# Second graph product of a two-layer graph network: panels of 512 columns instead of 384, column scale and step weights moved

## What is computed

```python
def _L1_gnn_ref(node_feats, adj_matrix, W, b):
    n = adj_matrix.shape[0]
    adj = adj_matrix + jnp.eye(n, dtype=adj_matrix.dtype)
    deg = jnp.sum(adj, axis=1)
    dinv = jnp.where(deg > 0, deg ** (-0.5), 0.0)
    adj_norm = dinv[:, None] * adj * dinv[None, :]
    x = node_feats @ W.T + b
    mean = jnp.mean(x, axis=0, keepdims=True)
    std = jnp.std(x, axis=0, ddof=1, keepdims=True)
    x = (x - mean) / (std + 1e-06)
    return adj_norm @ x

def step(h, _):                       # 30 times, in _L1_ffn_ref
    h = h + 0.01 * jnp.tanh(h)
    h = h * jax.nn.sigmoid(h)
    h = _layernorm(h, ln_w, ln_b)
    h = jnp.einsum('bsc,dc->bsd', h, W) + b
    return (h, None)

x = x + _L0_gnn_ref(_layernorm(x), adj, L0_gnn_W)
x = x + _L0_ffn_ref(_layernorm(x)[None], ...)[0]
x = x + _L1_gnn_ref(_layernorm(x), adj, L1_gnn_W, L1_gnn_b)
x = x + _L1_ffn_ref(_layernorm(x)[None], ...)[0]
```

## Time and profile before

| | us |
|---|---|
| median of 3 runs (2027.34 to 2028.16) | 2027.58 |
| the profiled execution | 2028.44 |
| its span, first to last instruction | 2026.7 |
| first graph product and experts, to | 860 |
| standardising, from 860 to | 926.5 |
| second graph product, from 926.5 to | 1184.5 |
| steps, from 1184.5 to | 2026.7 |

### The profile page before, as it was taken

The page is one execution under the profiler, slowest core; times in us unless marked ns, Lnnn a source line. Parts: engine busy times, 40 slices in busy tenths (PEclk is TensorE's granted clock), DMA queues, the critical chain, the costliest instruction groups (busy, mean ns, idle before and its releaser), DMA issues. The chain is left out here.

```text
span 2026.7 us, 44601 instructions
## 1 busy us (share of the span) xinstructions
PE 1816.9 (90%) x12898; PEld 1741.1 (86%) x12898; DVE 1650.8 (81%) x4233; ACT 1339.8 (66%) x2735; POOL 1035.0 (51%) x1756
## 2 busy tenths in 40 slices
PE   6468899919999999778999969999999999999998
PEld 4368899919999999767999959989998989999997
DVE  4888977738999999657666649989899989999897
ACT  4323455516666666345566649888888988889885
POOL 4543325444555555440000027777777777777774
PEclk9778999959999999988999989999999999999999
DMA  8755579427888788425666400000000000000001
GB/s 292 241 191 180 167 208 198 111 90 240 232 231 233 232 236 230 101 76 203 187 184 183 121 6 2 2 3 2 3 1 3 2 3 1 1 1 0 3 1 69
DMA packets 101001, 226.46 MB, mean 112 GB/s; under 512 B 21313, under 2 KB 51779, under 8 KB 92364
## 3 DMA queue, kind: packets, MB, share of 16 engines
q1 hardware_dynamic: 86220, 206.33, 32.7%
q0 software_dynamic: 14592, 17.91, 4.6%
HBM read 204.43 MB, written 19.75 MB: 111 GB/s over the span
## 5 line engine op out<-in xcount | busy, mean ns | idle before, releaser
L2341 PE MATMUL ffn_psH<-ffn_w2h,ffn_vTh 128*128 128x256 f32 x1320 | 406.2, 308 | 11.4 <-DVE ffn_vTl L2408 11.3
L2341 PE MATMUL ffn_psH<-ffn_w2h,ffn_vTl 128*128 128x256 f32 x1320 | 374.9, 284 | 0.0
L2341 PE MATMUL ffn_psH<-ffn_w2l,ffn_vTh 128*128 128x256 f32 x1320 | 374.0, 283 | 0.0
L2448 POOL TENSOR_SCALAR ffn_vn<-ffn_vn,ffn_rstd,ffn_shift 128x256 f32<-128x256 f32 x540 | 299.7, 560 | 20.2 <-issue 0.3
L2415 DVE SCALAR_TENSOR_TENSOR ffn_u<-ffn_th,ffn_psH 128x512 f32<-128x512 f32 x390 | 265.2, 680 | 49.2 <-ACT ffn_th L2368 49.0
L2403 DVE BATCH_NORM_STATS2 ffn_stats<-ffn_vn 128x6 f32<-128x256 f32 x780 | 281.8, 404 | 14.2 <-issue 11.9
L2341 PEld LDWEIGHTS ffn_psH<-ffn_w2h,ffn_vTh 128*128 128x128 f32 x1320 | 252.3, 191 | 35.2 <-DVE ffn_vTl L2408 18.2
L2371 ACT ACTIVATE ffn_vn<-ffn_u 128x512 f32<-128x512 f32 x390 | 254.8, 653 | 15.2 <-DVE ffn_u L2415 15.2
L2341 PEld LDWEIGHTS ffn_psH<-ffn_w2l,ffn_vTh 128*128 128x128 f32 x1320 | 253.6, 192 | 0.0
L2341 PEld LDWEIGHTS ffn_psH<-ffn_w2h,ffn_vTl 128*128 128x128 f32 x1320 | 252.7, 191 | 0.0
L2322 PE MATMUL ffn_psT<-ident,ffn_vn 128*128 128x128 f32 x1560 | 234.4, 273 | 9.1 <-POOL ffn_vn L2448 3.8
(11 more groups left out here) (244 smaller groups left out, 5205.2 us busy)
## 6 DMA issues: line engine op xcount, KB each, us to landing
g_raw<-in_adjt SPq DMA_DIRECT2D x272, 384.0 KB, 3.8
moe_w1raw<-in_wall SPq DMA_DIRECT2D x33, 1024.0 KB
moe_w2raw<-in_wall SPq DMA_DIRECT2D x33, 1024.0 KB, 5.8
g_raw<-in_adjl SPq DMA_DIRECT2D x27, 256.0 KB, 2.7
moe_b<-in_eb SPq DMA_DIRECT2D x33, 128.0 KB, 4.8
xn_rows<-rt_hn SPq DMA_DIRECT2D x8, 384.0 KB, 4.5
x_rows<-x SPq DMA_DIRECT2D x8, 384.0 KB, 6.4
out<-ffn_vn SPq DMA_DIRECT2D x12, 256.0 KB
```

What stands on the lines that cost most here:

```text
L2341: last = pe.matmul(psH[w % R][:, q * D:(q + 1) * D], a[:, w % R, q * KD + k, :], b[:, k, :], start=(k == 0 and j == 0), stop=(k == KD - 1 ...
L2448: last = pool.tensor_scalar(vn[:, t, :], vn[:, t, :], rstd[:, s:s + 1], shift[:, s:s + 1], ALU.mult, ALU.add)
```

## The change

`graph_block` is replaced by `second_graph_block`, written out without loops.

- Panels have 512 columns (WT = 4): six of them and one of 256. Chunks of two row tiles are 512 KB, in a ring of 10 buffers. The matrix is passed a second time, laid out for these panels (`wide`, `narrow`).
- SPLITS is 8.
- DVE adds the identity to the diagonal tiles of the loaded matrix, eight row tiles ahead; ACT's high part of such a tile waits for that. `plus_s` and its addition are gone.
- The features are scaled by `dinv` alone (`scale_z`), and both their parts are made by DVE, two row tiles ahead. The column scale is applied by ACT when it copies the accumulators out of PSUM (`evict`, a scale per partition). It is worked out in the first panel: PE turns the squares after row tile 6, DVE takes the variance at 12, POOL the root, DVE the reciprocal at 16.
- The result is scaled by `dinv` and added to x in one DVE instruction per row tile, read from PSUM.
- The weights of the steps are loaded behind the first chunk of the second panel and made in the second and third panel. `steps_block` gets them made.
- The normalised rows are written over z.

```diff
-def graph_block(nc, g, tag, adjt, adjl, s_row, dinv, column_scale, relu, hn, route=None):
+def second_graph_block(nc, g, wide, narrow, z, squares, weights, ffn):
+        WT = 4
+        WIDE = WT * P
+        PANELS = (NT + WT - 1) // WT
+        SPLITS = 8
+        RING = 10
...
+        TURNS = PANELS * NT
+        END = TURNS + 24
+        DIAGONAL = [p * NT + t for p in range(PANELS) for t in tiles_of(p)]
+        AHEAD = 8
+        def ended(m, after):
+            p = (m - after) // NT - 1
+            return p if (m - after) % NT == 0 and 0 <= p < PANELS else None
...
+        def _(sp):
+            for n in range(PANELS * CHUNKS):
+                p, c, r = n // CHUNKS, n % CHUNKS, n % RING
+                if n >= RING:
+                    sp.wait_ge(lo_done, (n - RING + 1) * CT)
+                if width(p) == WIDE:
+                    sp.dma_start(raw[:, r, :], wide[n * P:(n + 1) * P, :]).then_inc(loaded[r], 16)
...
+                if n == CHUNKS:
+                    sp.dma_start(wt[:], wt_in.rearrange("(k p) n -> p k n", p=P)).then_inc(w_loaded, 16)
...
+            def split_high(m):
+                p, n, v = m // NT, item(m), width(m // NT)
+                if m in DIAGONAL:
+                    act.wait_ge(diag_done, DIAGONAL.index(m) + 1)
+                else:
+                    act.wait_ge(loaded[n % RING], n // RING * 16 + 16)
+                if m >= SPLITS:
+                    act.wait_ge(mm_done, m + 1 - SPLITS)
+                act.activation(hi[:, m % SPLITS, 0:v], raw[:, n % RING, m % CT * v:(m % CT + 1) * v],
+                               ACT.Copy).then_inc(hi_done, 1)
+            def evict(p):
+                act.wait_ge(mm_done, (p + 1) * NT)
...
+                for d in range(KD):
+                    last = act.activation(out_t[:, d, 0:v], acc[p % 2][:, d, 0:v], ACT.Copy, scale=rinv[:, d:d + 1])
...
+            for m in range(END):                                    # ACT
+                if m < TURNS:
+                    split_high(m)
+                if ended(m, 6) is not None:
+                    evict(ended(m, 6))
+                if ended(m, 17) is not None:
+                    normalise(ended(m, 17))
...
+            def scale_z(t):
+                dve.tensor_scalar(sh[:, t, :], z[:, t, :], g.dinv1[:, t:t + 1], None, ALU.mult).then_inc(sh_done, 1)
+            def rest_of_z(t):
+                dve.wait_ge(sh_done, t + 1)
+                dve.scalar_tensor_tensor(out=sl[:, t, :], in0=z[:, t, :], scalar=g.dinv1[:, t:t + 1],
+                                         in1=sh[:, t, :].bitcast(F32), op0=ALU.mult, op1=ALU.subtract).then_inc(sl_done, 1)
+            def add_identity(m):
+                p, n = m // NT, item(m)
+                dve.wait_ge(loaded[n % RING], n // RING * 16 + 16)
+                a = m % CT * width(p) + (m % NT - p * WT) * P
+                dve.tensor_tensor(raw[:, n % RING, a:a + P], raw[:, n % RING, a:a + P], g.ident[:],
+                                  ALU.add).then_inc(diag_done, 1)
+            def add_to_x(p):
+                dve.wait_ge(tr_done, p + 1)
+                for i, t in enumerate(tiles_of(p)):
+                    last = dve.scalar_tensor_tensor(out=g.x[:, t, :], in0=psT[:, i, :], scalar=g.dinv1[:, t:t + 1],
+                                                    in1=g.x[:, t, :], op0=ALU.mult, op1=ALU.add)
+                last.then_inc(x_done, 1)
...
+            for t in range(2):
+                scale_z(t)
+            for t in range(2):
+                rest_of_z(t)
+            for m in range(AHEAD):
+                if m in DIAGONAL:
+                    add_identity(m)
+            for m in range(END):                                    # DVE
+                if m + AHEAD in DIAGONAL:
+                    add_identity(m + AHEAD)
+                if m < TURNS:
+                    split_low(m)
+                if m + 2 < NT:
+                    scale_z(m + 2)
+                    rest_of_z(m + 2)
+                if m == 12:
+                    variance()
+                if m == 16:
+                    column_scale()
+                if m == NT + 16:
+                    weights_first()
+                if m == NT + 22:
+                    weights_second()
+                if m == 2 * NT + 4:
+                    weights_rest()
+                if ended(m, 8) is not None:
+                    add_to_x(ended(m, 8))
+                if ended(m, 9) is not None:
+                    statistics(ended(m, 9))
+                if ended(m, 10) is not None:
+                    aggregate(ended(m, 10))
...
+            def contract(m):                                        # PE
+                p, j, b = m // NT, m % NT, m % SPLITS
...
+                pe.wait_ge(lo_done, m + 1)
+                for d in range(KD):
+                    fs = slice(d * P, (d + 1) * P)
+                    for r, (s, a) in enumerate(((sh, hi), (sh, lo), (sl, hi))):
+                        last = pe.matmul(acc[p % 2][:, d, 0:v], s[:, j, fs], a[:, b, 0:v], start=(j == 0 and r == 0),
+                                         stop=(j == NT - 1 and r == 2))
+                last.then_inc(mm_done, 1)
...
+            for m in range(END):
+                if m < TURNS:
+                    contract(m)
+                if m == 6:
+                    squares_by_feature()
+                if m == NT + 14:
+                    weight_sums()
+                if ended(m, 3) is not None:
+                    turn_back(ended(m, 3))
...
 def standardise_block: ends with
             dve.wait_ge(var_mm, G)
-            dve.tensor_copy(squares[:], psM[0:1, :]).then_inc(squares_done, 1)
...
-            dve.tensor_copy(scale[:], psM[:])
+            dve.tensor_copy(squares[:], psM[0:1, :])
...
-def steps_block(nc, g, wt_in, lw_in, lb_in, b_in, h0, out):
+def steps_block(nc, g, ffn, h0, out):
-            sp.dma_start(wt[:], wt_in.rearrange("(k p) n -> p k n", p=P)).then_inc(loaded, 16)
...
-            pe.wait_ge(w_ready, 3 * KD)
```

More of the change, by code:

```diff
@@ new lines, in second_graph_block @@
+        lbm = sb("ffn_lbm", [P, KD, P])
+        w2, w2h, w2l = ffn
+        wt_in, lw_in, lb_in, b_in = weights
+        acc = [ps(f"g1_acc{b}", [P, KD, 512]) for b in range(2)]
+        psT = ps("g1_psT", [P, WT, D])
+        psV = ps("g1_psV", [P, 512])
+        psW = ps("g1_psW", [P, 512])
+        loaded = [sem(f"chunk{r}") for r in range(RING)]
+        sh_done, sl_done = sem("sh"), sem("sl")
+        diag_done, hi_done, lo_done, mm_done = sem("diag"), sem("hi"), sem("lo"), sem("mm")
+        evicted, tr_done, x_done = sem("evicted"), sem("tr"), sem("x")
@@ L1177, in evict @@
                 last.then_inc(evicted, 1)
-            def scale(p, m):
-                n, _ = rows(p, m)
-                act.wait_ge(add_done, p)
-                act.wait_ge(dscale_done, p)
-                if m >= 2:
-                    act.wait_ge(x_done, p - 1)
-                for t in range(n):
-                    last = act.activation(delta[:, t, :], plus_s[:, t, :], ACT.Relu if relu else ACT.Copy,
-                                          scale=dscale[:, t:t + 1])
-                last.then_inc(act_done, 1)
@@ L1190, in normalise @@
-            def normalise(p, m):
-                n, _ = rows(p, m)
-                first = (p - 1) * PT
-                act.wait_ge(shift_done, p)
-                if route and m >= 2:
-                    act.wait_ge(stored, (p - 1) * 32)
-                    act.wait_ge(hback, p - 1)
-                for t in range(n):
-                    tile = slice(first + t, first + t + 1) if isinstance(p, int) else bass.ds(first + t, 1)
-                    to = hn[:, (m - 1) % 2, t:t + 1, :] if route else hn[:, tile, :]
-                    last = act.activation(to, g.x[:, tile, :], ACT.Identity, scale=rstd[:, t:t + 1],
-                                          bias=shift[:, t:t + 1])
-                last.then_inc(hn_done, 1)
@@ L1603, in _, with squares_by_feature, weight_sums @@
-            run(pe, panel, finish)
+            def squares_by_feature():
+                for d in range(KD):
+                    last = pe.matmul(psV[:, d:d + 1], squares[0:1, d * P:(d + 1) * P], g.ones[0:1, 0:1], start=True,
+                                     stop=True)
+                last.then_inc(psV_done, 1)
+            def weight_sums():
+                delta = psW[:, 0:D]
+                pe.wait_ge(lbm_done, 1)
+                for k in range(KD):
+                    pe.matmul(delta, lbm[:, k, :], wt[:, k, :], start=(k == 0), stop=False)
+                for k in range(KD):
+                    pe.matmul(delta, g.negones[:], wlw[:, k, :], start=False, stop=False)
+                pe.matmul(delta, g.ones[0:1, :], bias[0:1, :], start=False, stop=True).then_inc(delta_done, 1)
@@ L2038, in _ @@
                     statistics(2 + k // 2)
-            dve.memset(half[:], 0.5)
             dve.wait_ge(sum_done, 1)
@@ L2348, in _ @@
         def _(act):
-            act.wait_ge(w_ready, KD)
```

(2 more changed lines are left out.)

651 lines of the change are left out of this document (136 added, 515 removed).

## The result

The changed kernel takes 2017.5 us (median of five runs, 2013.7 to 2018.0) against 2027.6 for the kernel before (five runs, 2024.7 to 2028.2): the ratio is 0.9949, with a 95% interval of 0.9934 to 0.9963. The forecast was 2012.6, so the gain is 10 us instead of 15. The profiled execution took 2016.97 us with a span of 2015.2, against 2028.44 and 2026.7.

The account below looks back on a forecast made before the run. PE was taken to bound the product, and chains of waits its seams. Terms -3.8 + 3.0 - 3.9 + 2.6 - 0.7 - 1.35 - 11.2 + 0.4 = -15.0 took 2028.44 to 2013.5, 2012.6 beside the median; range 2005 to 2019, at 0.80.

Parts of the forecast that it names:

- The end of the standardising stage: Seam before the second product: column-scale work leaves the block, which then ends with the squares' copy at 921.80; -3.8 us.
- the head of the steps: Loads, weights, sums and w2 before the steps' first products move into the product, so PE starts at the barrier; -11.2 us.
- PE's stream: Second product's matmuls: 235.0 us becomes 231.2 with 512 columns at a pitch of 227 ns; -3.9 us.
- rival (a): PE's matmuls in the product: smaller fixed part at 512 columns, 215.8 ns, 10.5 us less, 2002; chance 0.06.
- Rival (b): Panel turn-overs of the product: DVE's wait for the transposes starves PE, 8.2 us lost, 2021; chance 0.06.
- Rival (d): First panel: DVE paces PE, scaling and rest taking 909 and 830 ns; 25.5 us lost, 2038; chance 0.03.
- the tie in the first panel: First panel of the product: DVE's 1.37 us per row tile against PE's 1.36, hence -0.7 us, ends -1.9 and +1.5.
- The sums: Sums of the steps' weights, added to PE in the product; with two matmuls of the squares +2.6 us, at most +4.7.
- The start of the product: First load to PE's first matmul: 8.0 against 4.99 us, waiting for the larger second chunk; +3.0, ends +1.6 and +3.4.
- the steps themselves: Last stage: steps left as they are; only the first products change, for clock and table load, +0.4 us, ends 0 and +1.
- Rival (c): Head of the steps: layer norm's chain paces the first round, so the 11 us come back; 2024; chance 0.03.

Follow-up runs that it names:

- e4: Changed kernel with the steps' weights made at the head of the steps as before, ScalarE's code placed three instructions later: 2023.2 us.
- f4: Changed kernel with second-product panels of 384 columns instead of 512, GpSimd's loop placed as by 100 more instructions: 2022.5 us.
- e1: Changed kernel with ScalarE's code three instructions later, by waits already met in the middle of the product: 2016.1 us.
- g1: Changed kernel with 2 more instructions in ScalarE's program and 34 in VectorE's, GpSimd's as changed: 2013.9 us.
- e3: Changed kernel with 2 more instructions in ScalarE's program, 34 in VectorE's and 100 in GpSimd's, all ahead of the steps: 2011.3 us.
- g2: Changed kernel with 34 more instructions in VectorE's program alone: 2017.2 us.
- e2: Kernel before with 61 more instructions at the start of ScalarE's program of the steps: 2028.7 us (2027.6 for the kernel before, beside it).
- f5: Kernel before with 123 more instructions at the head of GpSimd's steps (124 were meant): 2030.6 us (2028.4 beside it).

## Why the prediction was right, and where it was not

**The end of the standardising stage** and **the head of the steps** came out as worked out, to 0.3 us. The chain of waits had shown them as chains without other work beside them, so what left them left the time. e4 confirms the sum of the move from the other side: 11.5 us at the head less 2.8 in the product.

**PE's stream** came out for the reasons given. The pitch of 512 columns is 227 ns (23 pitches between 936.06 and 941.28), the straight line through the two pitches of the earlier trace rows, and not the 215.8 of rival (a), which is out. Rival (b) is out, since PE is busy for 200.00 of 200.00 us across the turn-overs. Rival (d) is out: scaling and rest took 0.35 and 0.48 us, the medians of the earlier trace rows. They did so in f4 too, and there VectorE sets PE's pace without (d)'s longer instructions (what made them longer in the first product, no run here tests), so the tie in the first panel that the prediction read from the earlier trace rows was a real one. The first panel took 2.8 us more than its 156 pitches, 3.5 before: the 0.7 that were forecast. The sums took 2.8 on PE, where 2.6 were forecast with the two matmuls of the squares.

**The start of the product** was mis-sized: +1.5 measured, +3.0 forecast. I had let the size of the chunks count, since the DMA engines were busy all through these microseconds, and took 6.7 us for the second chunk. VectorE was released by it 5.22 after the first load; with 384 KB ScalarE had been released at 5.35. Over the executions in which this wait shows it is 4.9 to 5.9 with 512 KB and 4.8 to 5.6 with 384, so what the size adds is less than the scatter, and 6.7 was not reached once. PE starts 6.1 to 7.1 after the first load with 512 KB, 1.1 to 2.1 more than the 4.99 before. The lower bound of the forecast, +1.6, was the right one.

**The step that failed is the steps themselves**: +0.4 forecast, +5.3 measured, of which some 4.5 are the place of the loop's code and some 0.8 go with GpSimd's longer instruction, which no run ties to the change. The prediction said that the rest of the steps "is left as it is the earlier trace rows", and took code that is not edited for code that takes the same time. It looked for effects of the change in the first round (clock, table load), priced them at 0.4 (from the first product to the first tanh 0.1 with the loop, 2.08 against 1.99 us, and 0.36 without), and never asked whether the loop behind it depends on something other than its instructions. It does: on where they lie. The page of the kernel before held the hint, VectorE's 11.9 us of "issue", a wait for nothing that the profile shows, at the jumps of a loop; I did not look at it because the steps weren't touched. That the time still lies within the stated range is luck: the range was made of other terms. Without the loop, the two kernels' steps are equally long, and the change is worth 17.7 us by the medians (2011.2 and 1993.5), 16.7 if each is set against the kernel before that ran beside it. From the squares' copy to the first product of the steps these two need 274.5 and 257.3 us, 17.2 apart.

Rival (c), that the head's gain comes back in the steps, had the right symptom, part of the gain given back there, and the wrong mechanism: the kernels without a loop show that nothing is given back for starting earlier, and in e4 the step with the jump is as long as in e1.

## What to carry to other kernels

A loop's time can change by an edit that doesn't touch it: before counting a later stage as unchanged, look for "issue" idle time at its loop edges, and reckon with some tenths of a microsecond to a few, a jump. Where two engines are late at one edge, removing one lateness shows nothing; judge by how the late engine's consumer moves, and take both away before clearing either. If the program has room, writing out a loop of a few long iterations is the first thing to try: here it gave more than the whole change.

## What the runs showed of the hardware

- After a jump back, ScalarE (324 instructions an iteration) and GpSimd (336) go on after 0.25 us or after 2.5 to 3.4, depending on where the loop lies; on ScalarE two instructions more ahead of it were enough to go from the one to the other (g1, e3). VectorE (469) was 2.8 to 3.5 us late, on the mean of six jumps, in every place in which it stood here. Whether there is a place for it without lateness was not tried.
- In some places a second lateness follows: 2.1 to 2.5 us on ScalarE, 0.3 to 0.6 on VectorE, where one packet of queue 14 a jump goes with it. That the loop's first instructions lie just ahead of a packet's end there is my reading of e1, g1 and g2, not a row of the trace, and not shown.
- PE's jump takes 0.2 us or 3.3 to 5.2, in one execution the one or the other from jump to jump (the kernel before, e2, f5, f4); a long one goes with nine packets of queue 8.
- The same normalising instruction of GpSimd takes 560 ns on the mean in six of the fourteen profiled executions and 563 or 564 in the other eight.
- The code ahead of the squares' copy, which the change leaves alone, reaches it between 916.6 and 923.8 us in the profiled executions of this study. That is more than most effects here, so I compared lengths between two marks of a trace, and the medians only after that.
